# A chain of six transformer blocks on one core: the transposed maxima in bf16, joint additions, retention scores in one step, and value products in any free bank

## The chip, the cores and the metric

The kernel runs on one core of a Trainium2 chip. The metric is the device time of one execution in microseconds; lower is better.

## What is computed

The input `x` is 16 batch entries of 256 tokens by 256 features. Each entry goes through six stages, each followed by a layer normalisation. Reduced to what matters:

```python
x = LN(x + attn0(x))            # 16 heads mixed within each token (linear attention), then a GELU MLP
x = LN(x + window_attn(x, ctx)) # softmax attention, 16 heads of 16, |query - key| <= 64
x = LN(x + cells(x))            # six chained softmax attentions, 8 heads of 32
x = LN(x + retention(x))        # out = q . cumsum(k v^T), 16 heads, causal, no softmax
x = LN(x + cross_attn(x, ctx, mask))  # softmax attention, 16 heads of 16, masked keys
x = LN(x + fourier_ffn(x))      # one 256 x 256 matrix in effect
```

Every softmax attention is `exp(s - max(s))` over 256 keys, its sum, and its product with the values.

## The kernel before

**Entries and slots.** Up to four entries are in flight (`NS = 4`, `s = i % NS`), each with its own SBUF slots; an entry starts when the one four before it has ended. An entry is a list of steps (`entry_steps`, from line 147). Each step names its engine, a duration, the steps that it needs, what it takes of PSUM (`takes`) and what it gives back (`frees`).

**The order.** `program_plan` (from line 323) plays the steps of all 16 entries through in list order of priority (the older entry first, then the longer tail, shaken by random numbers from `SEEDS`), and writes down the order of every engine and the banks that each step gets. The chip then runs these five fixed orders; semaphores alone hold it together. The durations in the list serve only to write the order. Among the kinds in `takes`, "misc" is any free bank, "score" a pair of banks (neighbours if there are any), "kept" a pair whose first bank stays taken until "rest", "half" one of the two halves of the probability buffer `pt` in SBUF, "ctx" a bank that is held long. PSUM has eight banks (`BANKS`). Where a step lacks what it wants, steps of lower priority that want the same kind are held back too.

**Attention in quads.** Four heads are one unit, `heads(n)` (line 207): `n` 0 to 3 are windowed (kind x), 4 to 15 belong to the cells (kind c), 16 to 19 are the masked cross attention (kind y). The steps of a unit are:
- `s` on TensorE: scores, queries by keys, each head with 32 contraction rows in a row group of its own and in a bank of its own. VectorE takes the negated maxima into `nmx` (L1257, for kind x L1251).
- `split` on VectorE: each f32 maximum is cut into three parts whose upper halves are bf16 numbers (L1263, L1266).
- `nm` on TensorE (L898): two f32 transposes of `nmx`, 128 by 128. ScalarE copies the result to SBUF (L1472).
- `st` on TensorE: the scores again, keys by queries (L911), and onto them the maxima as a product of three rows of ones with the three bf16 parts (L915). ScalarE takes the exponential (L1488) into `pt`. For kind c VectorE adds the two key blocks (L1275), for kind x GpSimd cuts the band (L1658).
- `pv` on TensorE (L942, L949): values by probabilities, and the sums. It is written into the first bank of the pair that the second exponential was read from; the bank is "kept" for this from the start of `st`. ScalarE and VectorE normalise and end its use (L1281, L1285, L1291, L1293, L1503).

An f32 product is two records in the trace.

**Retention.** For each of two feature blocks `f` there are two half steps `rs` (L1021), `(f, 0)` and `(f, 1)`: two heads each, for both parities and two token blocks, eight products of 128 columns. VectorE multiplies each half by the causal mask into `pt` (L1335). Then `rpv` (L1032, L1038) multiplies by the values, into a "ctx" bank. `r_state` (L1004) comes ahead.

**Elsewhere.** `features` (L750) and `tokens` (L742) are the 256 by 256 projections, `transposes` (L735) the transposes of activations, L853 the first MLP product. GpSimd's L1638 and L1648 are the products of the first attention.

## Time and profile before

| | before |
|---|---|
| three runs | 3463.22, 3470.81, 3472.40 us; median 3470.81 |
| profiled execution | 3470.35 us, its span 3468.6 us, mean granted TensorE clock 0.967 |
| TensorE matmuls busy | 3157.1 us (91%), 30860 records |
| weight loads (beside them) | 2362.2 us (68%) |
| VectorE | 2319.2 us (67%) |
| ScalarE | 1695.7 us (49%) |
| GpSimd | 1202.3 us (35%) |
| DMA | 122.9 MB, 35 GB/s |

Busy time is the union of an engine's instructions. Matmuls are pipelined and overlap each other, so what one costs is read from the distance between starts, and not from its duration. After some 400 us of setup and filling, the trace repeats itself every 202 to 204 us, once per entry, until some 3150 us.

### The profile page before, as it was taken

What the parts mean: (1) busy time and instruction counts of PE and PEld (TensorE: products, weight loads), DVE (VectorE), ACT (ScalarE), POOL (GpSimd) and SP (SyncE); (2) the same over time, 40 slices, a digit from 0 to 9 for tenths busy, and PEclk for the clock granted to TensorE, in tenths of its full rate; (3) what the DMA queues carried; (4) which work ended last, traced back from release to release, by engine and by line L of the source; (5) the groups of instructions that cost most, each with busy time, mean ns of one, the idle gap of its engine ahead of it and who ended that gap; (6) DMA issues with size and microseconds to landing.
All of it is one profiled execution on the core that took longest, in us unless ns stands there. A gap on an engine that the chain in (4) does not pass through costs nothing.

```text
span 3468.6 us, 77951 instructions
## 1 busy us (share of the span) xinstructions
PE 3157.1 (91%) x30860; PEld 2362.2 (68%) x30860; DVE 2319.2 (67%) x5004; ACT 1695.7 (49%) x3492; POOL 1202.3 (35%) x1308
## 2 busy tenths in 40 slices
PE   6889999999999999999999999999999999998866
PEld 5766666777676667667667776766777666666654
DVE  6676667667585776858677676867667585565533
ACT  1245464545546454454645545464544546454532
POOL 6886016162341606234160523416162341000000
PEclk8899999999999999999999999999999999999986
DMA  6211010010101001010100101010010101000000
GB/s 221 71 56 35 19 35 29 26 47 17 50 23 38 29 26 47 17 47 26 38 29 26 47 17 47 26 38 29 26 47 17 47 26 30 22 16 8 16 4 4
DMA packets 123283, 122.90 MB, mean 35 GB/s; under 512 B 9776, under 2 KB 122672, under 8 KB 122800
## 3 DMA queue, kind: packets, MB, share of 16 engines
q1 hardware_dynamic: 122928, 117.91, 11.2%
q8 instruction: 254, 4.16, 0.5%
q14 instruction: 101, 0.83, 0.1%
HBM read 113.69 MB, written 4.19 MB: 34 GB/s over the span
## 4 chain that ended last, share of the span: by engine, by line
PE 60%; DVE 16%; POOL 9%; issue 7%; ACT 6%; DMA 1%; SPq 1%; POOLq 0%; DVEq 0%; ACTq 0%
PE banks L750 17%; PE banks L742 13%; PE banks L888 7%; DVE nmx L1257 6%; PE banks L911 5%; PE banks L942 4%; POOL work L1648 4%; POOL work L1638 4%; ACT work L1488 3%; PE banks L1021 2%; PE banks L735 2%; PE banks L853 2%; DVE work L1218 2%; PE banks L898 1%; PE banks L949 1%
## 5 line engine op out<-in xcount | busy, mean ns | idle before, releaser
L750 PE MATMUL banks<-work,weights 128*128 128x256 f32 x3584 | 862.0, 388 | 19.4 <-DVE work L1281 13.5
L750 PEld LDWEIGHTS banks<-work,weights 128*128 128x128 f32 x3584 | 667.6, 192 | 161.3 <-issue 51.0
L1257 DVE TENSOR_REDUCE nmx<-banks 128x4 f32<-128x1024 f32 (+1 forms) x527 | 605.0, 1188 | 209.7 <-PE banks L888 209.3
L1488 ACT ACTIVATE work<-banks 128x1024 f32<-128x1024 f32 (+2 forms) x699 | 595.7, 913 | 281.5 <-PE banks L915 279.2
L742 PE MATMUL banks<-weights,work 128*128 128x256 f32 x2688 | 651.0, 388 | 29.9 <-DVE work L1281 12.3
L742 PEld LDWEIGHTS banks<-weights,work 128*128 128x128 f32 x2688 | 501.3, 193 | 132.9 <-issue 43.4
L1648 POOL TENSOR_TENSOR work<-work 128x512 f32<-128x512 f32 x256 | 400.1, 1582 | 202.2 <-DVE work L1218 105.1
L911 PE MATMUL banks<-work 32*128 32x256 f32 (+1 forms) x5120 | 395.2, 395 | 39.7 <-DVE nmx L1257 15.4
L888 PE MATMUL banks<-work 32*128 32x256 f32 (+1 forms) x5120 | 359.9, 396 | 67.1 <-ACT work L1390 37.6
L1638 POOL TENSOR_TENSOR work<-work 128x512 f32<-128x512 f32 x256 | 346.8, 1380 | 51.1 <-DVE work L1209 28.6
L1692 POOL TENSOR_TENSOR work<-work,row 128x512 f32<-128x512 f32 x64 | 107.6, 1681 | 731.0 <-PE banks L735 731.0
L942 PE MATMUL banks<-work 128*32 128x256 f32 (+3 forms) x5632 | 331.5, 356 | 25.2 <-DVE nmx L1257 16.6
L1275 DVE TENSOR_TENSOR added<-work 128x1024 f32<-128x1024 f32 x192 | 272.2, 1423 | 116.3 <-ACT work L1488 98.0
L888 PEld LDWEIGHTS banks<-work 32*128 32x128 f32 x5120 | 239.5, 189 | 152.8 <-issue 102.6
L911 PEld LDWEIGHTS banks<-work 32*128 32x128 f32 x5120 | 216.1, 190 | 173.5 <-issue 88.8
L1390 ACT ACTIVATE work<-banks,cb 128x256 f32<-128x256 f32 x384 | 161.0, 472 | 224.0 <-PE banks L750 224.0
L942 PEld LDWEIGHTS banks<-work 128*32 128x32 f32 x5632 | 153.6, 109 | 164.2 <-issue 83.9
L1218 DVE TENSOR_REDUCE work<-work 128x32 f32<-128x512 f32 x256 | 174.0, 682 | 126.3 <-POOL work L1648 124.4
L1658 POOL TENSOR_SCALAR_AFFINE_SELECT work<-work 128x128 f32<-128x128 f32 (+1 forms) x512 | 158.6, 356 | 285.6 <-ACT work L1488 285.6
L1214 DVE TENSOR_REDUCE work<-work 128x32 f32<-128x512 f32 x256 | 172.0, 682 | 121.9 <-POOL work L1638 121.8
L1472 ACT ACTIVATE work<-banks 128x256 f32<-128x256 f32 x320 | 119.0, 385 | 130.4 <-PE banks L898 130.0
L1251 DVE CUSTOM_DVE_ANT_0 banks<-banks,band 128x192 f32<-128x192 f32 x512 | 164.9, 393 | 19.9 <-PE banks L888 19.6
(160 smaller groups left out, 3753.2 us busy)
## 6 DMA issues: line engine op xcount, KB each, us to landing
weights<-in_w_all SPq DMA_DIRECT2D x322, 256.0 KB, 2.7
work<-in_w_setup SPq DMA_DIRECT2D x41, 256.0 KB, 5.8
work<-in_ctx SPq DMA_DIRECT2D x32, 256.0 KB, 3.0
work<-in_x SPq DMA_DIRECT2D x16, 256.0 KB, 2.9
out<-work SPq DMA_DIRECT2D x16, 256.0 KB, 2.2
weights<-in_w_all SPq DMA_DIRECT2D x1, 3072.0 KB, 12.8
row<-in_rows SPq DMA_DIRECT2D x1, 1280.0 KB, 9.2
mrow<-in_mask SPq DMA_DIRECT2D x16, 32.0 KB, 3.3
```

The source lines that it names most:

```text
L742: ins = e.matmul(b[:, m * 256:m * 256 + 256], xin[:, k, m * P:m * P + P], wslot(w)[:, k, :], start=(k == 0 and (m == 0 or closed)) if star ...
L750: ins = e.matmul(b[:, m * 256:m * 256 + 256], wslot(w)[:, k, m * P:m * P + P], xin[:, k, :], start=(k == 0 and (m == 0 or closed)) if star ...
L888: ins = e.matmul(b[g // 2][g % 2][:, cc * 256:cc * 256 + kk.stop - kk.start], q[32 * g:32 * g + 32, f, cc * P:cc * P + P], k[32 * g:32 * g ...
L911: e.matmul(b[g // 2][g % 2][:, o], k[32 * g:32 * g + 32, f, kc * P:kc * P + P], q[32 * g:32 * g + 32, f, qq], start=True, stop=False, tile ...
L942: ins = e.matmul(b[32 * g:32 * g + 32, lo:hi], left, right[:, kc * 256 + lo - qq.start:kc * 256 + hi - qq.start], start=(kc == 0), stop=(k ...
L1214: e.tensor_reduce(mix, big1, AX, ALU.add).then_inc(*tell(vec[s], "mix", a, i))
L1218: e.tensor_reduce(q, big2, AX, ALU.add).then_inc(*tell(vec[s], "mix sum", a, i))
L1257: ins = e.tensor_reduce(nmax(s, n)[:, 2 * p + j:2 * p + end, :], b.rearrange("p j (c n) -> p j c n", c=NC)[:, :, :, 0:w], AX, ALU.max, neg ...
L1275: e.tensor_tensor(added[:, half], pt(half, 0, 4)[:, :, 0:S], pt(half, 0, 4)[:, :, S:2 * S], ALU.add).then_inc(*tell(vec[s], "added", a, i))
L1488: ins = e.activation(dst, b.rearrange("p j (c n) -> p j c n", c=NC)[:, :, :, 0:w], ACT.Exp)
L1638: e.tensor_tensor(big1, q.unsqueeze(2).broadcast_to([P, PH, NH, DH]), k.unsqueeze(1).broadcast_to([P, PH, NH, DH]), ALU.mult).then_inc(*te ...
L1648: e.tensor_tensor(big2, mix.unsqueeze(2).broadcast_to([P, PH, DH, NH]), v.unsqueeze(1).broadcast_to([P, PH, DH, NH]), ALU.mult).then_inc(* ...
```

## The change

Five edits:
- `nm`: the two f32 transposes become two bf16 products of the upper halves of `nmx` (a strided view) with a bf16 identity. The results are stored as bf16, densely.
- `st` of kinds c and y: the scores of both key blocks come first, and then each head has one addition of 512 columns (the maxima are read twice by a broadcast) where there were two of 256. For kind x the order stays. The first product of a bank alone carries the start flag.
- `st` takes two plain pairs; both banks of each are free after the exponential. `pv` takes any free bank as it starts, and its readers free that.
- `rs`: one step per feature block, four heads, sixteen products; it takes a half, two pairs and a "ctx" bank at once.
- The listed durations of six steps, and the five seeds, are others, so that the order of every engine and the banks are written anew.

```diff
-SEEDS = (271952, 450768, 66414, 843758, 204716)
+SEEDS = (452137, 292473, 324644, 23518, 278264)
...
-        maxed = [do("DVE", "s", (n, p), 1.13, b, frees=((b, p),)) for p in range(2)]
+        maxed = [do("DVE", "s", (n, p), 1.13 if kind != "x" else 1.21, b, frees=((b, p),)) for p in range(2)]
...
-        b = do("PE", "nm", n, 0.22, *maxed, *((st_done[n - 2],) if n >= 2 else ()), takes=("misc",))
+        b = do("PE", "nm", n, 0.16, *maxed, *((st_done[n - 2],) if n >= 2 else ()), takes=("misc",))
...
-        s = st_done[n] = do("PE", "st", n, 1.12 if kind != "x" else 1.0, nm, 
+        s = st_done[n] = do("PE", "st", n, 1.2 if kind != "x" else 1.08, nm, 
...
-                            takes=("score", "kept", "half"))
+                            takes=("score", "score", "half"))
...
-            e = [do("POOL", "band", (n, p), 1.0, e[p]) for p in range(2)]
+            e = [do("POOL", "band", (n, p), 1.22, e[p]) for p in range(2)]
         pv = do("PE", "pv", n, 1.3 if kind == "c" else 0.9, *e, *both, v,
-                frees=((s, 2),))
+                takes=("misc",), frees=((s, 2),))
         if par == 0:
-            part[n] = do("ACT", "part", n, 0.7, pv, frees=((s, "rest"),))
+            part[n] = do("ACT", "part", n, 0.7, pv, frees=((pv, 0),))
...
-        p0 = do("PE", "rs", (f, 0), 0.87, r_q_t, *((("PE", "rs", (f - 1, 0)),) if f else ()), takes=("half", "score", "ctx"))
-        m0 = do("DVE", "rs", (f, 0), 1.22, p0, frees=((p0, 1),))
-        p1 = do("PE", "rs", (f, 1), 0.87, p0, takes=("score",))
-        m1 = do("DVE", "rs", (f, 1), 1.22, p1, frees=((p1, 0),))
...
+        p = do("PE", "rs", f, 0.95, r_q_t, *((("PE", "rs", f - 1),) if f else ()), takes=("half", "score", "score", "ctx"))
+        m = [do("DVE", "rs", (f, j), 1.22, p, frees=((p, 1 + j),)) for j in range(2)]
...
+        def nmax_parts(s, n, c):
+
+            return small[s]["nmx"].bitcast(BF16)[:, n % 2, c].rearrange("p (n h) -> p n h", h=2)[:, :, 1]
...
         def stored_nmax(s, n):
-            return slot(s, NMT[quad(n)[0]])[:, n % 2, :]
+            return slot(s, NMT[quad(n)[0]])[:, n % 2, :].bitcast(BF16)[:, 0:S]
...
-                        ins = e.transpose(b[:, c * P:c * P + P], small[s]["nmx"][:, a % 2, c, :], ident[:, :])
+                        ins = e.matmul(b[:, c * P:c * P + P], nmax_parts(s, a, c), ident_bf[:, :], start=True, stop=True)
...
-                                     q[32 * g:32 * g + 32, f, qq], start=True, stop=False,
+                                     q[32 * g:32 * g + 32, f, qq], start=(kc == 0), stop=False,
...
+                    if kind != "x":
                         for g in range(4):
-                            ins = e.matmul(b[g // 2][g % 2][:, o], added_row[32 * g:32 * g + 3, :],
-                                           upper(stored_nmax(s, a))[32 * g:32 * g + 3, qq], start=False,
-                                           stop=True, tile_position=(32 * g, 0))
-                            if kc == NC - 1 and g == 1:
+                            ins = e.matmul(b[g // 2][g % 2].rearrange("p (c n) -> p c n", c=NC), ones_bf[32 * g:32 * g + 3, :],
+                                           stored_nmax(s, a)[32 * g:32 * g + 3, :].unsqueeze(1).broadcast_to([3, NC, S]),
+                                           start=False, stop=True, tile_position=(32 * g, 0))
+                            if g == 1:
...
-                    picked[:] = [home["exp", a, 1, i][0]]
-                    b = take("ctx", "norm", a, i)
+                    b = take("misc", "norm", a, i)
...
-                    b = take("score", "rm", f, p, i)
-                    if p == 0:
-                        take("ctx", "rout", f, i)
+                    book(i, f"r{a}")
+                    b = [take("score", "rm", a, 0, i), take("score", "rm", a, 1, i)]
+                    take("ctx", "rout", a, i)
                     for par in range(2):
                         for c in range(NC):
-                            for j in range(2):
-                                g = 2 * p + j
...
+                            for g in range(4):
```

## Rows read from the trace of the kernel before

**Rows 1.** The page: busy time by engine, and the chain that ended last.

```profile
PE 3157.1 (91%) x30860; PEld 2362.2 (68%) x30860; DVE 2319.2 (67%) x5004; ACT 1695.7 (49%) x3492; POOL 1202.3 (35%) x1308
...
PE 60%; DVE 16%; POOL 9%; issue 7%; ACT 6%; DMA 1%; SPq 1%; POOLq 0%; DVEq 0%; ACTq 0%
```

**Rows 2.** Busy time by stage: stretch, its length, then each engine, clock, DMA.

```profile
400.00:3150.00 2750.00, 2573.38 (x26040) 1914.74 (x26038) 1914.26 (x4170) 1431.37 (x2960) 927.34 (x1026) 0.99 0.11 31
3150.00:3469.00 319.00, 242.58 (x2244) 175.68 (x2244) 146.08 (x266) 122.82 (x249) 10.28 (x13) 0.86 0.03 8
...
1431.00:1633.00 202.00, 189.92 (x1903) 141.25 (x1902) 142.53 (x309) 105.20 (x218) 74.74 (x79) 0.98 0.11 33
```

**Rows 3.** TensorE's waits in the whole run: total us, times, longest.

```profile
PE banks L888 <- ACT work L1390: 37.6, 35, 2.3
...
PE banks L888 <- DVE nmx L1257: 24.1, 34, 1.5
PE banks L1021 <- DVE work L1335: 17.9, 13, 1.5
PE banks L942 <- DVE nmx L1257: 16.6, 13, 1.3
PE banks L911 <- DVE nmx L1257: 15.4, 34, 1.2
```

**Rows 4.** Groups by line and shape: busy, mean ns of one, idle before.

```profile
L898 PE MATMUL banks<-ident,nmx 128*128 128x128 f32 x640 | 124.4, 291 | 43.0 <-DVE nmx L1266 27.9 <-DVE nmx L1257 11.7 <-DVE nmx L1251 0.3
...
L898 PEld LDWEIGHTS banks<-ident,nmx 128*128 128x128 f32 x640 | 74.9, 143 | 109.2 <-issue 53.5 <-DVE nmx L1266 45.1
...
L915 PEld LDWEIGHTS banks<-work,ones_bf 3*128 3x128 bf16 x2048 | 64.3, 94 | 4.6
```

**Rows 5.** TensorE in order of time (start, us): transposes of maxima, what follows.

```profile
1525.85 0.60 PE L898 MATMUL banks<-ident,nmx 128*128 128x128 f32 x4
1526.29 3.62 PE L742 MATMUL banks<-weights,work 128*128 128x256 f32 x16
```

**Rows 6.** TensorE in order of time: the second half of an `st` step.

```profile
1530.49 0.61 PE L911 MATMUL banks<-work 32*128 32x256 f32 x8
1530.92 0.30 PE L915 MATMUL banks<-work,ones_bf 3*128 3x256 bf16 x4
1531.04 0.61 PE L911 MATMUL banks<-work 32*128 32x256 f32 x8
```

**Rows 7.** TensorE in order of time: retention scores at the full clock.

```profile
1229.85 1.05 PE L1021 MATMUL banks<-work 32*128 32x128 f32 x14
1230.63 0.48 PE L888 MATMUL banks<-work 32*128 32x256 f32 x2
1230.73 0.28 PE L1021 MATMUL banks<-work 32*128 32x128 f32 x2
1230.84 1.03 PE L888 MATMUL banks<-work 32*128 32x256 f32 x14
1231.80 0.44 PE L898 MATMUL banks<-ident,nmx 128*128 128x128 f32 x2
1233.72 3.33 PE L1021 MATMUL banks<-work 32*128 32x128 f32 x48 [1.48 <-DVE work L1335]
1236.98 0.71 PE L1032 MATMUL banks<-work 128*128 128x128 f32 x4
```

**Rows 8.** The same stretch by engine, and a later entry's at a lower clock.

```profile
1229.50:1237.00 7.50, 6.02 (x87) 5.00 (x85) 7.43 (x15) 0.77 (x3) 2.53 (x2) 1.00 0.11 37
...
1638.00:1643.00 5.00, 4.71 (x50) 4.28 (x51) 5.00 (x8) 0.00 (x0) 0.00 (x0) 0.73 0.00 0
...
1638.29 4.25 PE L1021 MATMUL banks<-work 32*128 32x128 f32 x48 [1.48 <-DVE work L1335]
1642.47 1.22 PE L1032 MATMUL banks<-work 128*128 128x128 f32 x4
```

**Rows 9.** VectorE's masking of retention scores, in order of time.

```profile
1232.32 1.26 DVE L1335 TENSOR_TENSOR work<-banks,causal 128x512 f32<-128x512 f32 x2
```

More of the change, by code:

```diff
@@ L361, in pick @@
                 found = [0] if long_held[0] < LONG else []
-            elif kind in ("score", "kept"):
+            elif kind == "score":
                 found = sorted(((u, v) for u in range(BANKS) for v in range(u + 1, BANKS) if bank_left[u] and bank_left[v]),
@@ L382, in mark @@
             bank[u[0]] = bank[u[1]] = is_free
-        elif kind == "kept":
-            bank[u[1]] = is_free
-            bank[u[0]] = False
-        elif kind == "rest":
-            bank[u[0]] = True
         elif kind == "misc":
@@ L905, in tensor @@
                     e.wait_ge(*when("nm", a, i))
-                    added_row = minus_bf if kind == "x" else ones_bf
                     for kc in range(NC):
@@ L1008, in tensor @@
                 elif op == "rs":
[L1009 to L1010 removed]
+                    if a == 0:
                         e.wait_ge(*when("r_q_t", i))
[L1012 to L1016 removed]
+                    book(i, f"r{a}")
+                    b = [take("score", "rm", a, 0, i), take("score", "rm", a, 1, i)]
+                    take("ctx", "rout", a, i)
                     for par in range(2):
                         for c in range(NC):
[L1019 to L1023 removed]
+                            for g in range(4):
+                                ins = e.matmul(b[g // 2][g % 2][:, par * S + c * P:par * S + c * P + P],
+                                               slot(s, XT)[32 * g:32 * g + 32, a, c * P:c * P + P],
+                                               slot(s, R_QT[par])[32 * g:32 * g + 32, a, c * P:c * P + P],
                                                start=True, stop=True, tile_position=(32 * g, 0))
[L1025 removed]
+                                if par == 1 and c == 1 and g == 1:
+                                    ins.then_inc(*tell(pe[s], "rs mm", a, 0, i))
+                    ins.then_inc(*tell(pe[s], "rs mm", a, 1, i))
                 elif op == "rpv":
```

24 lines of the change are left out of this document (10 added, 14 removed).

## The prediction

> **What bounds the kernel now.** I read the page's busy shares first. The reader is to see one engine far ahead of the others: TensorE's matmuls are busy for 3157 of 3468.6 us, 91%, and the chain that ended last lies on TensorE for 60% of the span, on VectorE for 16% [rows 1]. Then the busy time by stage: between 400 and 3150 us matmuls are busy for 2573 of 2750 us, 94%, and in one period of 202 us (one batch entry goes in and one comes out) for 189.9 us; VectorE has 142.5 us in the same period, ScalarE 105, GpSimd 75 [rows 2]. So a microsecond of TensorE work taken out of an entry should shorten the run by nearly a microsecond, as long as the 12 us of idle time in a period do not grow. In the last 319 us TensorE is busy for 243 only; there latency counts, not work. Last I read who ended TensorE's waits: no single cause is large, and the largest are inputs of a score product (37.6 us over the run), the row maxima that VectorE takes out of banks (24.1, 16.6 and 15.4 us ahead of three kinds of product), and the retention products' banks (17.9 us) [rows 3].
>
> The sum below is made against the profiled execution, 3470.35 us (span 3468.6); the median of the three runs is 3470.81, so they are the same to 0.5 us.
>
> **Transposes of the maxima.** There are 20 `nm` steps in an entry, 320 in all (640 records [rows 4]). Two such steps in a row start at 1525.85 and the next operation at 1526.29: 0.44 us, 0.22 us each [rows 5]. Each is two f32 transposes of 128 columns. The new step has two bf16 products of 128 columns. No row shows a bf16 product over the whole array. From below, the bf16 additions stream 4 products of 256 columns, on four row groups at once, in 0.12 us, so one product of 128 columns cannot be put at less than 0.06 us: 0.12 us a step [rows 6]. From above, the step stays at 0.22 us if its two weight loads set its pace: 143 ns is one f32 load now, and 94 ns one bf16 load of three rows [rows 4]. Two loads of 94 ns, half covered, give some 0.16 us. I take that, 0.06 us less a step: 320 x 0.06 = **19 us** (0 to 32). Nothing argues for a loss. The Trainium skill (TensorE: Matmul & The Clock Gate, Back-to-back issue gap) puts an isolated bf16 product of 128 columns at 55.6 ns; by that the step would be 0.11 us and the saving 35 us, and no row here shows it.
>
> ScalarE's copy of the result now writes bf16; I count nothing, since ScalarE is busy for 105 of 202 us [rows 2].
>
> **Joint additions.** In the 256 `st` steps of the kinds c and y, the products of one key block take 0.43 us (1530.49 to 1530.92) and its four additions 0.12 us [rows 6]. Afterwards there are two blocks of products, 0.86 us, and four additions of 512 columns. These cost 0.24 us if each costs twice one of 256, and 0.21 us if only the columns count (512 at 2.4 GHz). The step goes from 1.10 us to between 1.07 and 1.10. I take 0.02 us: 256 x 0.02 = **5 us** (0 to 8). The 64 steps of kind x keep all their instructions, and the dense bf16 maxima that they now read are no fewer columns.
>
> **Retention scores in one step.** Now there are four half steps per entry, each with two row groups. In the period at 1229 us the first starts at 1229.85 and gives way at 1230.73, 0.88 us; a score step and a transpose of other entries come between; then TensorE idles 1.48 us until VectorE's masking of the first half has emptied banks, and the other three halves take until 1236.98, 3.26 us [rows 7]. The joint step has the same columns on four row groups: 32 records of 128 columns, against 16 of 256 in a score step, of which the last 14 take 0.96 us (1230.84 to 1231.80) [rows 7]. I put it at 1.05 us. Pure work: 4 x 0.88 - 2 x 1.05 = 1.4 us an entry, 16 x 1.4 = **23 us**. Around it lie stalls: the idle 1.48 us (17.9 us over the run [rows 3]); 3.26 - 3 x 0.88 = 0.6 us by which the later halves are drawn out, 10 us over 16 entries; and in about nine entries the same three halves take 4.18 us (1638.29 to 1642.47) [rows 8], 0.9 us more, 8 us. In that stretch the granted clock is 0.73 in the mean, so partly at the lower of its two levels (1.2 GHz), after TensorE had idled 1.48 us and gone on with two row groups [rows 8]. Together 36 us. They do not all go. VectorE still has four maskings for each step, 2.5 us (two take 1.26 us) [rows 9], and is busy for 7.43 of the 7.50 us around it now [rows 8]; the second joint step must wait for banks that these empty, and is late by 2.5 us unless other entries' products fill that. I take a third: **12 us** (from -20 to 36; below nothing, because a step now claims four score banks and one for its output at once, five of eight).
>
> **Value product in any bank.** It has the same instructions, so no TensorE work moves. A bank that was kept from the start of `st` to the end of the normalisation is now free from the exponential to the value product, and the value product has to find one free. What covers it is that it claims one bank and not a pair, and that the normalisation empties it soon. If it waits instead, `co`, the next score step and all behind it on TensorE wait as well, and with them ScalarE's normalisation. The nearest rows are today's waits of products for maxima in banks, 16.6 and 15.4 us over the run [rows 3]. So I bound this between -30 us (most of rows 3's bank waits go) and +15 us (as many again come), and take 0.
>
> **The order.** All five engines' orders are written out anew with other costs and other seeds. Every step may move, weight streaming on SyncE's queue with it (its loads follow the starts of products), and GpSimd's bands and additions. No row prices that. TensorE's 12 us of idle time per period are what an order can win or lose; I allow 1 us a period either way, 15 us, and take 0.
>
> Sum: 19 + 5 + 23 + 12 = 59 us, 3470.35 - 59 = **3411 us**; 3390 to 3432 as this case's own range, from the order's 15 us and the transposes' bounds.
>
> **Rivals.** *VectorE bounds the retention stretch.* For: it is busy for 7.43 of 7.50 us there [rows 8], and its eight maskings, 5.0 us an entry, are not touched. Against: TensorE has products of three other entries to put in between, and VectorE has 59 us of slack in a period [rows 2]. Then only the 24 us of transposes and additions are won: 3446 us. The Trainium skill states this as a rule (TensorEngine Tiling (Array Packing), PSUM Bottleneck): tiling speeds up TensorE, and emptying PSUM may become the bottleneck.
>
> *More comes back.* If the freed bank removes half of the 56 us of waits on L1257, and the other 24 us of retention stalls go too: 3411 - 28 - 24 = 3359 us.
>
> *Everything is returned as idle time,* because the latency of one entry's chain (exponentials, sums, GpSimd's products) sets the period and not TensorE: 3470 us. Against it speaks 94% busy; for it that 40% of the chain is not on TensorE [rows 1, 2].
>
> *Slower: the five banks.* A joint step starts only when two pairs, one more bank and a half of the probability buffer are free together. Under the list order lower steps that want pairs are held back for it, and single banks go on being taken by others. This decides from 59 / 32 = 1.8 us of TensorE idle time per joint step on. Today a half step that wants two banks idles 1.48 us [rows 7]; were it VectorE's whole time for a step, 2.5 us, the bill is 32 x 2.5 = 80 us, and the run takes 3411 + 80 = 3491 us. Against: in the steady stretch TensorE nearly always finds something else.
>
> **How the numbers follow.** The forecast, 0.45. VectorE bounds retention, 0.20 (the row of 7.43 in 7.50 is strong but local). More comes back, 0.12. All returned, 0.10. Five banks or a worse order, 0.13. A measurement of this kernel tells about 0.3%, 10 us, from no change. Faster by more: 0.45 + 0.20 + 0.12 = 0.77; within: 0.10; slower: 0.13. The range goes from 3370, which leaves out half of "more comes back" (0.06), to 3470, above which lie the slower case and a little of "all returned" (0.13 to 0.15).
>
> **What would show it.** Of the transposes: `nm` steps 0.16 us apart, not 0.22. Of the additions: 1024 records of 512 columns, 0.21 to 0.24 us per four. Of retention: two blocks of 32 records, each about 1.05 us, and no idle 1.48 us ahead of them; were the rival right, products of retention would be preceded by idle time ended by VectorE's masking. Of the banks: value products with no wait for an eviction. Overall: matmuls busy for some 3110 us (3157 - 47), and idle time in a period still near 12 us. I am wrong if idle time grows by what the work shrinks, or if the order's share, put at 0, is larger than any of the terms.

## The result and the profile after

The change made the kernel slower.

| | before | after |
|---|---|---|
| median of the runs | 3469.39 us | 3507.49 us (3497.86 to 3515.63) |
| ratio to before | | 1.0108 [1.0085, 1.0132] |
| profiled execution, its span | 3470.35, 3468.6 us | 3515.63, 3513.9 us |
| mean granted TensorE clock | 0.967 | 0.957 |
| TensorE busy / idle in the span | 3157.1 / 311.5 us | 3127.5 / 386.4 us |

The forecast was 3411 us, with 3370 to 3470 as its range. The median lies 96 us above the one and 37 us above the other. The profiled execution after is the longest of its four, 8 us above their median, so differences between the two profiles are some 7 us larger than those between the medians (38.1 us).

The page of the kernel after, busy time and the chain that ended last, as [rows 1]:

```profile
PE 3127.5 (89%) x29836; PEld 2321.7 (66%) x29836; DVE 2362.6 (67%) x5022; ACT 1695.1 (48%) x3504; POOL 1189.7 (34%) x1308
...
PE 54%; DVE 19%; POOL 9%; issue 9%; ACT 6%; DMA 2%; SPq 1%; DVEq 0%; POOLq 0%; ACTq 0%
```

TensorE works 29.6 us less, and idles 74.9 us more; together 45.3 us, the difference of the two spans. In the chain its part falls from 60% to 54% of the span (some 2080 to 1900 us), VectorE's rises from 16% to 19% (some 555 to 670 us), and the part in which an engine waited for nothing that the profile shows rises from 7% to 9% (some 243 to 316 us). VectorE is also busy for 43.4 us more, though the change gives it no new work.

The busy time by stage, as [rows 2] (stretch, length, then busy time and instructions of TensorE, weight loads, VectorE, ScalarE and GpSimd, granted clock, DMA share, GB/s). The last one is a period of the kernel after:

```profile
400.00:3150.00 2750.00, 2490.61 (x24399) 1839.78 (x24398) 1911.12 (x4085) 1390.49 (x2895) 906.04 (x993) 0.97 0.11 31
...
1439.00:1646.00 207.00, 186.98 (x1835) 137.98 (x1834) 144.53 (x303) 105.44 (x219) 74.78 (x79) 0.98 0.11 32
```

So the time is lost in the steady stretch: there TensorE's idle time goes from 177 to 259 us. Between 825 and 2905 us the same retention step returns every 208.0 us in the mean, where it returned every 202.6 us; a period has 20 us of idle time and not 12.

TensorE's groups of the kernel after, with the idle time just ahead of them and what ended it, as the first line of [rows 4]:

```profile
L891 PE MATMUL banks<-ident_bf,nmx 128*128 128x128 bf16 x640 | 88.1, 226 | 82.2 <-DVE nmx L1254 47.9 <-DVE nmx L1263 22.7 <-ACT work L1485 6.8
...
L1016 PE MATMUL banks<-work 32*128 32x128 f32 x1024 | 45.9, 326 | 30.6 <-DVE work L1332 22.6 <-DVE nmx L1254 8.1
```

Ahead of the `nm` steps TensorE now idles for 82.2 us, where it was 43.0 us [rows 4]: the very step that became cheaper has 39 us more idle time ahead of it. Ahead of retention scores it is 30.6 us, for 18 before [rows 3].

### The profile page after: what moved, and what is told of

The parts are those of the page before. It is cut to its first block, busy times and chain, and to the rows that moved or that the text cites. A ratio compares the mean times of both kernels' runs of the same rounds, so it can differ in the third digit from the quotient of the medians.

```text
span 3513.9 us, 75891 instructions
## 1 busy us (share of the span) xinstructions
PE 3127.5 (89%) x29836; PEld 2321.7 (66%) x29836; DVE 2362.6 (67%) x5022; ACT 1695.1 (48%) x3504; POOL 1189.7 (34%) x1308
## 4 chain that ended last, share of the span: by engine, by line
PE 54%; DVE 19%; POOL 9%; issue 9%; ACT 6%; DMA 2%; SPq 1%; DVEq 0%; POOLq 0%; ACTq 0%
PE banks L743 14%; PE banks L735 12%; DVE nmx L1254 6%; PE banks L903 6%; PE banks L881 5%; PE banks L941 5%; POOL work L1645 5%; POOL work L1635 3%; ACT work L1485 3%; DVE work L1195 2%; PE banks L846 2%; DVE added L1272 2%; PE banks L728 2%; PE banks L948 1%; DMA mrow<-in_mask 1%
## 5 line engine op out<-in xcount | busy, mean ns | idle before, releaser
L743 PE MATMUL banks<-work,weights 128*128 128x256 f32 x3584 | 848.4, 386 | 12.3 <-DVE work L1278 6.5
L1254 DVE TENSOR_REDUCE nmx<-banks 128x4 f32<-128x1024 f32 (+1 forms) x545 | 605.9, 1154 | 242.4 <-PE banks L881 240.8
L1485 ACT ACTIVATE work<-banks 128x1024 f32<-128x1024 f32 (+3 forms) x711 | 599.5, 899 | 265.7 <-PE banks L915 238.3
L735 PE MATMUL banks<-weights,work 128*128 128x256 f32 x2688 | 671.8, 397 | 44.3 <-DVE work L1278 28.7
L735 PEld LDWEIGHTS banks<-weights,work 128*128 128x128 f32 x2688 | 509.7, 196 | 159.8 <-issue 51.8
L1645 POOL TENSOR_TENSOR work<-work 128x512 f32<-128x512 f32 x256 | 407.3, 1606 | 36.2 <-DVE work L1215 19.1
L881 PE MATMUL banks<-work 32*128 32x256 f32 (+1 forms) x5120 | 356.6, 397 | 61.3 <-ACT work L1485 28.2
L903 PE MATMUL banks<-work 32*128 32x256 f32 (+1 forms) x5120 | 369.2, 398 | 40.4 <-ACT work L1469 18.3
L1635 POOL TENSOR_TENSOR work<-work 128x512 f32<-128x512 f32 x256 | 359.7, 1414 | 118.4 <-DVE work L1211 103.2
L1272 DVE TENSOR_TENSOR added<-work 128x1024 f32<-128x1024 f32 x192 | 271.2, 1412 | 164.7 <-ACT work L1485 161.0
L941 PE MATMUL banks<-work 128*32 128x256 f32 (+3 forms) x5632 | 334.2, 359 | 45.4 <-ACT work L1485 24.9
L881 PEld LDWEIGHTS banks<-work 32*128 32x128 f32 x5120 | 241.4, 190 | 154.2 <-issue 103.3
L903 PEld LDWEIGHTS banks<-work 32*128 32x128 f32 x5120 | 237.0, 190 | 146.8 <-issue 88.7
L1689 POOL TENSOR_TENSOR work<-work,row 128x512 f32<-128x512 f32 x64 | 89.2, 1394 | 608.9 <-PE banks L728 608.8
L1469 ACT ACTIVATE work<-banks 128x256 bf16<-128x256 f32 x320 | 121.5, 388 | 251.4 <-PE banks L891 251.3
L1211 DVE TENSOR_REDUCE work<-work 128x32 f32<-128x512 f32 x256 | 171.1, 678 | 55.0 <-POOL work L1635 54.8
L1677 POOL MEMSET work<- 128x512 f32 x16 | 8.4, 525 | 554.9 <-PE banks L1035 554.9
```

The lines of the kernel that those rows point to most:

```text
L735: ins = e.matmul(b[:, m * 256:m * 256 + 256], xin[:, k, m * P:m * P + P], wslot(w)[:, k, :], start=(k == 0 and (m == 0 or closed)) if star ...
L743: ins = e.matmul(b[:, m * 256:m * 256 + 256], wslot(w)[:, k, m * P:m * P + P], xin[:, k, :], start=(k == 0 and (m == 0 or closed)) if star ...
L881: ins = e.matmul(b[g // 2][g % 2][:, cc * 256:cc * 256 + kk.stop - kk.start], q[32 * g:32 * g + 32, f, cc * P:cc * P + P], k[32 * g:32 * g ...
L903: e.matmul(b[g // 2][g % 2][:, o], k[32 * g:32 * g + 32, f, kc * P:kc * P + P], q[32 * g:32 * g + 32, f, qq], start=(kc == 0), stop=False, ...
L941: ins = e.matmul(b[32 * g:32 * g + 32, lo:hi], left, right[:, kc * 256 + lo - qq.start:kc * 256 + hi - qq.start], start=(kc == 0), stop=(k ...
L1211: e.tensor_reduce(mix, big1, AX, ALU.add).then_inc(*tell(vec[s], "mix", a, i))
```

## The experiments

Two theories stood against each other at first. *The mechanics:* the joint retention step, the banks or the bf16 products cost more than forecast. *The order:* the edits are worth what the sum says, but the orders that are written out anew are worse by more. The median of the kernel before lay between 3468.35 and 3471.66 us in each series of measurements below, so times of different series can be compared to some 3 us. Some kernels below change `SEEDS` alone, and so only the written order; their computation stays the same. For each the table further down gives the makespan as well, the end of the play-through that `program_plan` itself comes to.

**The cheaper products alone, in the order of before.** The bf16 transposes and the joint additions are put into the kernel before; the list of steps, its durations and the seeds stay, so every engine keeps its order.

```diff
-    ins = e.transpose(b[:, c * P:c * P + P], small[s]["nmx"][:, a % 2, c, :], ident[:, :])
+    ins = e.matmul(b[:, c * P:c * P + P], nmax_parts(s, a, c), ident_bf[:, :], start=True, stop=True)
...
-    q[32 * g:32 * g + 32, f, qq], start=True, stop=False,
+    q[32 * g:32 * g + 32, f, qq], start=(kc == 0), stop=False,
...
-    ins = e.matmul(b[g // 2][g % 2][:, o], added_row[32 * g:32 * g + 3, :],
+    ins = e.matmul(b[g // 2][g % 2].rearrange("p (c n) -> p c n", c=NC), ones_bf[32 * g:32 * g + 3, :],
```

> The kernel before with the order of every engine and all banks held as they were; only the products of nm (bf16) and st (joint additions) are those of the change. Theory A, the new order lost the time and the products are cheaper as forecast: 24 to 40 us less than before, 3430 to 3446 us, with nm steps 0.13 us apart in place of 0.22. Rival B, the new products themselves cost time (a lower granted clock, a drain ahead of bf16): 3470 us or more. Rival C, the saved work turns into waits whatever the order: 3460 to 3475 us with more idle time on TensorE.

Measured: 3468.78 us, ratio 0.9995 [0.9982, 1.0008]. The page and the steady stretch of this kernel:

```profile
PE 3134.8 (91%) x29836; PEld 2334.6 (67%) x29836; DVE 2317.9 (67%) x5004; ACT 1695.9 (49%) x3492; POOL 1204.1 (35%) x1308
...
400.00:3150.00 2750.00, 2553.11 (x25154) 1891.56 (x25152) 1913.22 (x4172) 1430.22 (x2957) 928.86 (x1026) 0.98 0.11 31
```

TensorE's busy time falls by 22.3 us, 20.3 of them in the steady stretch, where as much idle time takes its place. The 24 us of these two terms are worth nothing in this order. In a fixed order the engine cannot take other work when its next input has not arrived. That is the result of the rival "everything is returned as idle time", for these two edits in a held order; that the latency of one entry's chain is the reason, as that rival says, is not shown. The clock moved as well: the mean granted clock is 0.961 to 0.963 in the ten runs and 0.962 to 0.968 in those of the kernel before beside them, and in the stretch shown it is 0.98 where it was 0.99 [rows 2]. The two edits do not explain the loss either, so it lies in the retention step, the banks or the order.

**The seeds exchanged.** The kernel before gets the seeds of the kernel after, and the other way round.

```diff
-SEEDS = (271952, 450768, 66414, 843758, 204716)
+SEEDS = (452137, 292473, 324644, 23518, 278264)
```

> The kernel before with the five new seeds and nothing else: the same instructions in another order. Theory A (an order is worth tens of microseconds): the makespan that the order writer itself comes to is 3490.2 in place of 3359.5, so some 130 us slower, about 3600 us. Rivals B and C, for which the order is nothing: within 15 us of before, 3455 to 3485 us.

> The changed kernel with the five old seeds. Theory A: the order writer comes to 3465.4 in place of 3373.7, so some 90 us slower than the changed kernel, about 3600 us. Rival D, the claims of the joint retention step and of the value product are what costs, whatever the seeds: within 15 us of the changed kernel, 3490 to 3525 us.

**No seeds.** Both kernels with `SEEDS = ()`, where nothing shakes the priorities: the first order that the rule alone gives.

> The kernel before with no seeds: the partner of the changed kernel with no seeds, which took 3560 us (1.027 of before). The order writer comes to 3457.6 here and to 3435.9 there. Theory A, the change shortens the run where neither order was picked: slower than that partner, 3570 to 3620 us. Theory D, its claims cost as much as its instructions save: 3560 us or less.

> The changed kernel with no seeds at all, so that the order follows the plain tails and nobody has picked it. To be read against the kernel before with no seeds, e4. The order writer comes to 3435.9 here and 3457.6 there. Theory A: some 3570 us, and 20 to 60 us less than e4. Rival D: as slow as e4 or slower.

**Seeds sought anew for both.** For each kernel 2100 orders were written, and the one with the shortest makespan was run.

> The changed kernel with eight other seeds, found as the best of 2100 orders by the makespan that the order writer itself comes to: 3326.5 where the recorded seeds come to 3373.7 and the kernel before to 3359.5. On the five kernels run so far, 1 us of that makespan is about 1.3 us on the chip. Theory A, the change is sound and its seeds were not: 3425 to 3460 us, faster than both. Theory D, the claims of the new steps cost on the chip what the writer does not see: 3480 us or more.

> The kernel before with three other seeds, the best of 2100 orders by the writer's makespan (3375.9), the same effort as for the changed kernel, whose best was 3326.5 and took 3453 us. Theory A: 3480 to 3520 us, slower than the kernel before, whose recorded seeds (3359.5) are a lucky find, and slower than the changed kernel with its searched seeds. Theory D: 3455 us or less.

Measured, sorted by makespan (us):

| list of steps | seeds | makespan | time | ratio to before |
|---|---|---|---|---|
| after | best of 2100 | 3326.5 | 3453.34 | 0.996 [0.9946, 0.9975] |
| before | its own | 3359.5 | 3469.39 | 1 |
| after | its own | 3373.7 | 3507.49 | 1.0108 [1.0085, 1.0132] |
| before | best of 2100 | 3375.9 | 3519.30 | 1.0132 [1.0114, 1.0149] |
| after | none | 3435.9 | 3560.31 | 1.0266 [1.0227, 1.0305] |
| before | none | 3457.6 | 3598.67 | 1.0361 [1.0343, 1.0379] |
| after | those of before | 3465.4 | 3613.42 | 1.0417 [1.0382, 1.0451] |
| before | those of after | 3490.2 | 3640.69 | 1.0495 [1.0467, 1.0523] |

The searched and unshaken runs came out in the ranges expected; of the exchanges, for which I had some 3600 us each, that of the kernel before is 41 us slower than that. Four things follow. The order alone moves the time by 171 us (3469 to 3641), and I had allowed it 15. Seeds chosen for one list did harm in the other: either kernel is slower with the other's seeds than with none. The makespan ranks all eight as the chip does; over the whole table 163.7 us of makespan are 187.4 us on the chip. And the kernel before had an unusually good order: 2100 orders of its list hold none with so short a makespan (3375.9 against 3359.5), and the best of them takes 49.9 us longer than its own.

The loss can be split along these runs, in two ways. Without seeds the change saves 3598.67 - 3560.31 = 38.4 us. Its own seeds bring the kernel before 3598.67 - 3469.39 = 129.3 us, and the kernel after only 3560.31 - 3507.49 = 52.8 us, 76.5 us less. -38.4 + 76.5 = 38.1 us, which is the result. With one search of the same length for each, the change saves 3519.3 - 3453.3 = 66 us; counted from there the two kernels' own seeds make 104 us of difference. So the edits are worth 38 to 66 us in orders that they had an even chance in, and the orders that the two kernels came with lose 76 to 104 us. That the sum had 59 does not confirm its terms: below, the cheaper products give 0 and 11 us where it had 24.

By the rival of the five banks the new list would be the slower one in both pairs, since the joint step claims its banks in every order of it. It is the faster in both. That the claims cost something within the 38 and 66 us is not excluded.

**Where part of the order's idle time comes from: the split of the maxima.** In the trace after, one `split` instruction of VectorE that usually takes 0.17 us takes 3.11 us. VectorE, GpSimd and TensorE in order of time (start, duration, engine, line, operation, and for TensorE the idle time ahead and its end):

```profile
1367.54 0.68 DVE L1211 TENSOR_REDUCE work<-work 128x32 f32<-128x512 f32 x1
1368.13 3.11 DVE L1260 TENSOR_TENSOR nmx<-nmx 128x8 f32<-128x8 f32 x1
1371.28 0.18 DVE L1263 TENSOR_TENSOR nmx<-nmx 128x8 f32<-128x8 f32 x1
1371.37 1.22 DVE L1254 TENSOR_REDUCE nmx<-banks 128x4 f32<-128x1024 f32 x1
...
1367.30 1.49 POOL L1645 TENSOR_TENSOR work<-work 128x512 f32<-128x512 f32 x1
1368.76 2.45 POOL L1635 TENSOR_TENSOR work<-work 128x512 f32<-128x512 f32 x2
...
1372.73 0.37 PE L891 MATMUL banks<-ident_bf,nmx 128*128 128x128 bf16 x2 [3.75 <-DVE nmx L1254]
```

GpSimd multiplies in three instructions back to back from 1367.30 to 1371.21, and the 8-column subtraction ends only then. The maxima of the next unit (L1254) stand behind it on VectorE and free a bank at 1372.59; `nm` starts at 1372.73, after TensorE has idled for 3.75 us. The first reduction, 0.68 us, runs beside GpSimd without delay. Seven periods of the steady stretch have such a gap of 3.7 to 3.8 us. In four others the same instruction gets its turn between two of GpSimd's, the second one is held instead, and the gap is 2.1 to 2.4 us:

```profile
1577.71 0.71 DVE L1260 TENSOR_TENSOR nmx<-nmx 128x8 f32<-128x8 f32 x1
1578.46 1.17 DVE L1263 TENSOR_TENSOR nmx<-nmx 128x8 f32<-128x8 f32 x1
...
1576.87 1.52 POOL L1645 TENSOR_TENSOR work<-work 128x512 f32<-128x512 f32 x1
1578.34 2.47 POOL L1635 TENSOR_TENSOR work<-work 128x512 f32<-128x512 f32 x2
```

TensorE's clock behind the gap at 1369 us (same columns as above):

```profile
1368.00:1371.00 3.00, 0.99 (x17) 0.58 (x15) 3.00 (x2) 0.00 (x0) 3.00 (x3) 1.00 0.00 0
1371.00:1374.00 3.00, 1.26 (x4) 0.98 (x5) 2.96 (x5) 0.38 (x1) 0.21 (x1) 0.57 0.00 0
1374.00:1377.00 3.00, 3.00 (x8) 2.37 (x7) 2.93 (x7) 0.00 (x0) 0.05 (x1) 0.50 0.00 0
```

The granted clock is 1.00 while the engine falls idle, and 0.57 and 0.50 (the lower level, 1.2 GHz) in the next two stretches, although TensorE is busy for all of the last one.

To take the suspected cause away, the two subtractions are replaced by instructions of the same size that read one operand, so that the lower two parts of the maxima stay zero (`nmx` is set to zero at the start); this leaves out the lower two parts of every maximum. All five orders are held. It is done in the kernel after and in the kernel before.

```diff
-    e.tensor_tensor(nmax(s, a, 1), nmax(s, a, 0), nmax_upper(s, a, 0), ALU.subtract)
+    e.tensor_reduce(nmax(s, a, 1), nmax(s, a, 2).unsqueeze(3), AX, ALU.max)
...
-    e.tensor_tensor(nmax(s, a, 2), nmax(s, a, 1), nmax_upper(s, a, 1), ALU.subtract)
+    e.tensor_reduce(nmax(s, a, 2), nmax(s, a, 1).unsqueeze(3), AX, ALU.max)
```

> The changed kernel, its order held; the two small VectorE instructions that split the maxima (two SBUF inputs, 0.17 us alone, up to 3.11 us while GpSimd multiplies) become instructions with one SBUF input. Leaves out: the two lower parts of the maxima, which stay zero, so that the maximum that is subtracted is rounded to bf16. Theory P, VectorE and GpSimd share a port and this makes part of the 43 us that VectorE is busier: the longest split falls from 3.1 to 0.2 us, the 3.75 us gap of TensorE in each period goes, the low-clock stretch behind it too, 25 to 60 us less than the changed kernel: 3447 to 3482 us. Theory O, the order's waits alone cost: 3500 to 3510 us.

> The same edit in the kernel before, its order held, leaving out the same lower parts of the maxima. Theory P: the splits are held far less here (longest 1.27 us), so 0 to 12 us less than before, 3458 to 3470 us, and the changed kernel gains at least twice as much from the edit. Theory O: 3465 to 3472 us, and both gain the same.

Measured: after 3457.73 us, ratio 0.9974 [0.996, 0.9989], 49.8 us less than the kernel after; before 3434.18 us, ratio 0.9917 [0.9892, 0.9942], 35.2 us less than the kernel before. The two splits as groups (busy us, mean ns, idle ahead): first in the kernel after, then with one operand; and the same line's shortest, median and longest in ns in both:

```profile
L1263 DVE TENSOR_TENSOR nmx<-nmx 128x8 f32<-128x8 f32 x320 | 83.0, 260 | 11.0
L1260 DVE TENSOR_TENSOR nmx<-nmx 128x8 f32<-128x8 f32 x320 | 80.3, 251 | 5.8 <-issue 0.3
...
L1260 DVE TENSOR_TENSOR nmx<-nmx x320: 159/170/3140, 140.3 to 3484.9; 128x8 f32<-128x8 f32 x160
```

```profile
L1263 DVE TENSOR_REDUCE nmx<-nmx 128x8 f32<-128x8 f32 x320 | 54.0, 169 | 11.0
L1260 DVE TENSOR_REDUCE nmx<-nmx 128x8 f32<-128x8 f32 x320 | 51.9, 162 | 5.9 <-issue 0.3
...
L1260 DVE TENSOR_REDUCE nmx<-nmx x320: 151/161/171, 146.6 to 3436.0; 128x8 f32<-128x8 f32 x160
```

A median of 170 and a longest of 3140 ns become 161 and 171: the holds are gone, 57 us of VectorE's time, for 50 us of the run. The gaps of 3.7 us in the steady stretch are gone with them, and `nm` has 47.1 us of idle time ahead of it where it had 82.2:

```profile
L891 PE MATMUL banks<-ident_bf,nmx 128*128 128x128 bf16 x640 | 87.4, 225 | 47.1 <-DVE nmx L1263 19.0 <-DVE nmx L1254 17.9 <-ACT work L1485 6.8
```

Of the 48.9 us between the two profiled spans, TensorE's idle time makes 25.8 and its busy time 23.1 (3127.5 to 3104.4 us for the same products), while the mean clock rises from 0.957 to 0.966.

In the kernel before the same two lines are busy for 128.8 us, so the holds were there too and smaller, and taking them away is worth 35 us. I had put that at 12 us at most, and expected the changed kernel to gain at least twice as much: two misses. The difference, 14.5 us, is the part of the 38 us that this one contention explains, and it is loose: by the ratios the gains are 46 and 29 us, and the intervals allow some 13 us either way. The written order knows nothing of the contention, and the new one puts more splits beside GpSimd's products: 40 of the 640 take over 0.3 us, before 20. But the holds do not rank orders. In the searched order, 54 us faster, the splits are held longer still, 170.2 us for 163.3:

```profile
L1260 DVE TENSOR_TENSOR nmx<-nmx 128x8 f32<-128x8 f32 x320 | 107.6, 336 | 9.4
L1263 DVE TENSOR_TENSOR nmx<-nmx 128x8 f32<-128x8 f32 x320 | 62.6, 196 | 11.1 <-DVE nmx L1260 0.2
```

**The low clock at the second retention step.** In the kernel after the second joint step runs at the lower clock in nine of the 16 entries, here for its whole length:

```profile
1242.44 1.17 PE L1016 MATMUL banks<-work 32*128 32x128 f32 x32 [0.74 <-DVE nmx L1254]
1243.55 0.28 PE L891 MATMUL banks<-ident_bf,nmx 128*128 128x128 bf16 x2
1245.55 2.09 PE L1016 MATMUL banks<-work 32*128 32x128 f32 x32 [1.72 <-DVE work L1332]
1247.57 0.80 PE L1029 MATMUL banks<-work 128*128 128x128 f32 x2
```

The first takes 1.11 us (1242.44 to 1243.55), the second 2.02 us, after 1.72 us of idle time that VectorE's masking ended. To see what the low clock costs, TensorE is given extra products into the output's bank ahead of each joint step, so that it does not stand idle there.

```diff
...
+    spare = take("ctx", "rout", a, i)
+    for _ in range(3 if a else 1):
+        e.matmul(spare[:, 0:S], slot(s, XT)[:, a, 0:P], slot(s, XT)[:, a, 0:S], start=True, stop=True)
...
```

> The changed kernel, its order held, with f32 products of 128x256 that nobody reads ahead of the two joint retention steps, one before the first and three before the second, in the bank that the step's output gets later: they fill the gaps of 0.7 and 1.7 us in which TensorE waits there for VectorE. Theory G, the gaps bring the lower clock for what follows: the second joint step takes 1.1 us in place of 1.9 to 2.1 in every entry, the low-clock time in the steady stretch falls from 150 to about 110 us, and the run is 5 to 20 us faster than the changed kernel, 3487 to 3502 us. If the clock does not answer to this: the same or up to 15 us slower, by the products themselves where the gaps are short.

Measured: 3506.39 us, ratio 1.0113 [1.0098, 1.0128]; no different from the kernel after. The clock did come back. The stretch around the second step and the step itself:

```profile
1238.00:1244.00 6.00, 5.63 (x108) 4.50 (x108) 5.86 (x14) 0.38 (x1) 0.00 (x0) 1.00 0.01 3
...
1241.26 1.17 PE L1020 MATMUL banks<-work 32*128 32x128 f32 x32
1242.36 0.71 PE L1033 MATMUL banks<-work 128*128 128x128 f32 x4
```

The second step takes 1.10 us (1241.26 to 1242.36) at a granted clock of 1.00, all 32 joint steps now take 1.10 or 1.11 us, and the run's mean clock rises from 0.957 to 0.967 (0.963 to 0.967 in its four runs, where the kernel after has 0.957 to 0.964). The time stays, where I had expected 5 to 20 us less. VectorE is busy for 5.86 of these 6.00 us, which fits that the stretch waits for it and that a faster TensorE there ends nothing sooner. So the low clock at this step did not make the kernel slower. For the rest of the run that is not shown: the extra products are work themselves (64, at 0.50 us each where three take 1.49 us), the mean clock between 400 and 3150 us came back in part only (0.97, now 0.98; before 0.99), and within the kernel after the slowest run has the lowest clock (3515.63 us at 0.957) and the fastest the highest (3497.86 us at 0.964).

**Do cheap products pay where the order suits them?** *Work* (Theory W below): they pay once the holds on VectorE are gone. *Held order* (Theory H): they pay only in an order that was written for them. For the one, the edits of the first experiment are put on the kernel before with one-operand splits (lower two parts left out here too). For the other, the searched order of the kernel after is held, and the old f32 transposes and the two additions of 256 columns are put back under it.

```diff
-    ins = e.matmul(b[:, c * P:c * P + P], nmax_parts(s, a, c), ident_bf[:, :], start=True, stop=True)
+    ins = e.transpose(b[:, c * P:c * P + P], small[s]["nmx"][:, a % 2, c, :], ident[:, :])
...
-    ins = e.matmul(b[g // 2][g % 2].rearrange("p (c n) -> p c n", c=NC), ones_bf[32 * g:32 * g + 3, :],
+    ins = e.matmul(b[g // 2][g % 2][:, o], added_row[32 * g:32 * g + 3, :],
```

> The kernel before, its order held, with the bf16 transposes and joint additions and with the splits of the maxima that have one SBUF input (leaves out the two lower parts of the maxima). The one-input splits alone took 3434 us, the cheaper products alone 3469. Theory W, the products' saving was hidden because transposes wait for VectorE's splits, which GpSimd holds: 3405 to 3425 us. Theory H, an order written for the old durations has no place where this saving counts, held splits or not: 3428 to 3440 us.

> The changed kernel with the searched seeds (3453 us), its order held, but with the f32 transposes and the two additions of the kernel before: everything else of the change stays. Theory H, the products' cost counts in an order that was written for the cheap ones: 20 to 40 us slower than 3453, 3473 to 3493 us. If the cheaper products are worth nothing in any order: 3445 to 3465 us, and the change's gain is all of the retention step and the banks.

Measured: 3439.17 us, ratio 0.9917 [0.9895, 0.9939], where the same kernel without them has 3434.18; and 3464.77 us, ratio 0.9989 [0.9976, 1.0002], where the searched order with the new products has 3453.34. In the order written for the old list they are worth nothing even without holds, so *Work* fails. In the searched order of the new list they are worth 11.4 us, about half of the 24 us that the sum gave them; the runs do not overlap (3449.84 to 3456.5 against 3457.89 to 3470.25 us). But 3464.77 us is below the 3473 to 3493 of *Held order* and in the range that I had given for products worth nothing in any order. And the new list is not one of cheaper products throughout: it has `nm` at 0.16 for 0.22 and `st` at 1.20 for 1.12. So what is shown is that the same edit is worth nothing in one order and some 11 us in another; that the list's durations make the difference is not.

One rival was not taken apart from this: in each of the three pairs the kernel with the cheaper products has the lower clock in its profiled run (0.963 for 0.967 in the first experiment, 0.965 for 0.974 and 0.959 for 0.962 here), so part of the saved work may have gone into slower products.

**The best of both.** The searched order with one-operand splits; and then the split step taken out of the list and the code altogether, `nm` waiting for the maxima themselves, at 0.14 us in the list, with the best of some 12000 orders. Both leave out the lower two parts of the maxima.

```diff
-        maxed = [do("DVE", "split", n, 0.36, *maxed)]
-        b = do("PE", "nm", n, 0.16, *maxed, *((st_done[n - 2],) if n >= 2 else ()), takes=("misc",))
+        b = do("PE", "nm", n, 0.14, *maxed, *((st_done[n - 2],) if n >= 2 else ()), takes=("misc",))
```

> The changed kernel with the eight searched seeds and the splits of the maxima with one SBUF input (leaves out the lower two parts of the maxima, which stay zero). If the port's share and the order's add up: 3453 less 30 to 50 us, 3405 to 3425 us. If the search already avoids what the port costs: 3440 us or more.

> The changed kernel without the split at all: the transposes start from the maxima, the lower two parts stay zero (left out), the step is gone from the list, and the seeds are the best of some 12000 orders, makespan 3290.8. By 1.3 us on the chip for each us of makespan against the kernel before: 3380 us; 3370 to 3410 us, faster than both kernels.

Measured: 3398.54 us, ratio 0.9781 [0.9761, 0.98]; and 3396.05 us, ratio 0.9775 [0.9756, 0.9794], makespan 3290.8. One-operand splits are worth 54.8 us on top of the searched order, more than I had expected (30 to 50). The second kernel is faster than before by more than 2%, the first is just at that mark; both are over 3% below the kernel after. The second brings next to nothing over the first, though its makespan is 36 us shorter: the list prices a split at 0.36 us, and on the chip the two take 0.33 us once nothing holds them. So between these two the makespan did not tell the time; what became of those 36 us is open.

## Why the prediction was wrong

**The order, put at 0 and bounded by 15 us, is the step that failed.** "TensorE's 12 us of idle time per period are what an order can win or lose; I allow 1 us a period" takes the idle time that a good order leaves as a measure of what a bad one can cost. It bounds what a better order could still win, and says nothing of what a worse one loses. Measured, the order is worth 76 to 104 us between the two kernels with their own seeds, and 171 us for one kernel with other seeds. The prediction's last sentence named this case ("if the order's share, put at 0, is larger than any of the terms"); it is the one that came, with "idle time grows by what the work shrinks": busy time fell by 29.6 us and idle time grew by 74.9.

**The premise that a microsecond of TensorE work is nearly a microsecond of time failed as well.** It rests on 94% busy. Taking 22 us of work out without moving anything gave 0.9995 [0.9982, 1.0008]. The 94% is an average over five fixed orders that wait for one another, and in both kernels only 54 to 60% of the chain lies on TensorE.

**A reading of the waits was wrong.** The prediction calls 37.6 us and then the maxima and the retention banks TensorE's largest waits. Two of the three largest are left out there, behind two small VectorE instructions, the scaling of the layer normalisation and the split:

```profile
PE banks L735 <- DVE work L1198: 29.0, 7, 14.1
PE banks L898 <- DVE nmx L1266: 27.9, 21, 4.5
```

So the prediction never asked what these two cost. The waits alone would not have told: with one-operand splits the second is still 25.9 us, and the kernel before gains 35 us all the same.

**The terms, one by one.**
- *Transposes, 0.22 to 0.16 us.* Right in kind, the size too small. One step starts at 1237.78 and what follows at 1237.91: 0.13 us, at the lower bound (0.12) and not at the value taken. At 0.09 us less a step the term would be 29 us; with the additions that makes 34 us, and TensorE's busy time fell by 22.3 us in the first experiment.

```profile
1237.78 0.29 PE L891 MATMUL banks<-ident_bf,nmx 128*128 128x128 bf16 x2
1237.91 0.61 PE L728 MATMUL banks<-ident,work 128*128 128x128 f32 x4
```

- *Joint additions, 0.21 to 0.24 us per four.* Right: 0.22 us (1504.26 to 1504.48), in 1024 records.

```profile
1504.26 0.40 PE L915 MATMUL banks<-work,ones_bf 3*128 3x512 bf16 x4
1504.48 1.04 PE L903 MATMUL banks<-work 32*128 32x256 f32 x16
```

- *Retention work, 1.05 us a step.* 1.11 us at the full clock, so 4 x 0.88 - 2 x 1.11 = 1.3 us an entry and not 1.4. The second step of an entry takes 1.70 to 2.02 us in the nine entries in which it meets the low clock.
- *Retention stalls, a third of 36 us gained.* Wrong in sign. The idle time that VectorE's masking ends ahead of these products went from 17.9 us [rows 3] to 22.6, and 8.1 us behind maxima came on top. This is the mechanism of the rival of VectorE as the bound, which I gave 0.20, though its time (3446 us) is 61 us too low; the sentence of the Trainium skill (TensorEngine Tiling (Array Packing), PSUM Bottleneck) that it was weighed with holds here: the masking is what the second step waits for, 1.72 us in the entry shown. The extra products fit it: TensorE's speed at that step was worth nothing.
- *Value product in any bank, 0 between -30 and +15 us.* Its waits behind maxima fell from 16.6 us [rows 3] to 2.5, and those of the second scores from 15.4 us [rows 3] to 7.3. But value products now wait 24.9 us for the exponentials (before 7.7), and `nm` 47.9 us behind maxima (before 11.7). The waits moved on; which of it is the bank and which the order was not taken apart.

TensorE's waits in the kernel after (us in total, times, longest), as [rows 3]:

```profile
PE banks L891 <- DVE nmx L1254: 47.9, 26, 3.8
PE banks L728 <- DVE work L1195: 36.0, 17, 14.2
...
PE banks L941 <- ACT work L1485: 24.9, 44, 1.1
PE banks L891 <- DVE nmx L1263: 22.7, 16, 4.2
PE banks L1016 <- DVE work L1332: 22.6, 14, 1.8
```

- *Matmuls busy for some 3110 us.* 3127.5: 29.6 us less work, where 47 were forecast.

**The five banks,** the rival that ended on the other side, gave a time near the result (3491 us) for a reason that does not hold: without seeds and with searched seeds the new list is faster than the old, by 38 and 66 us. That the rival's number lies 16 us from the median is luck.

**What stays open.** The retention step and the free bank were not run apart, so how the 38 to 66 us divide between them is not shown. "Best of 2100" is one draw for each kernel, and 66 us have that draw in them. The listed durations changed together with the code, and no run tells the two apart. Some 14.5 of the 38 us, give or take 13, are holds on the splits; the rest of what makes the new order worse is known only as its makespan, 14.2 us longer than that of before, and the part of the clock in it is open.

## What to carry to other kernels

Where every engine runs an order that a planner wrote, a change of the planner's list is two changes: price the edit with both orders sought with equal effort, and give the order a range taken from a few other seeds, not from today's idle time. The planner's own makespan is cheap, and it ranked eight orders here without a mistake; it knows nothing of what the list leaves out, such as holds (50 us at the same makespan). And a small instruction between two engines' queues is worth a look at its longest, not its median: instructions of 0.17 us, some of them held for up to 3.1 us, cost 50 us of the run, more than the cheaper products gave in any order.

## What the runs showed of the hardware

**A two-operand VectorE instruction is held while GpSimd works, and sometimes does not get its turn between GpSimd's instructions.** The subtraction of 8 columns waited through the rest of one product of 1.49 us and two more, 2.45 us together, that GpSimd ran without a gap; 3.11 us for 0.17. In other periods of the same trace it got its turn after the first product, 0.71 us at 1577.71; what decides between the two is not known. Of the 40 splits that take over 0.3 us, 39 end within 0.1 us after a GpSimd instruction ends. Reductions with one operand in SBUF ran beside them at 0.68 us, and as a replacement for the subtraction never took more than 172 ns. The Trainium skill (SBUF — State Buffer, "SBUF: two separate sides") states the lock: a VectorE instruction with two SBUF operands and a GpSimd instruction that reads SBUF exclude each other for their whole length. The trace agrees. By the same section whichever starts first keeps the pair for its instruction, which alone would bound a hold here by the rest of one product, under 1.5 us; the measured 3.1 us is the longer, and the measurement decides. The hold works the other way too: 38 of the 256 products of L1635 take over 1.5 us (median 1.27), and 37 of them overlap VectorE's addition of L1272, which has two operands.

**The scaling of the layer normalisation is held in the same way.** Its group in the kernel after, against 97.7 us and 428 ns in the kernel before:

```profile
L1195 DVE TENSOR_SCALAR work<-work,mv,rstd 128x256 f32<-128x256 f32 x256 | 145.0, 608 | 15.5 <-ACT rstd L1396 15.4
```

It is the same instruction 256 times, 47 us longer in all, and one-operand splits leave it as it is (144.1 us). Most of the 256 keep to the median of 411 ns; 55 take over 0.6 us, before 8, and 54 of the 55 end within 0.2 us after a GpSimd instruction ends. Two in a row:

```profile
1389.59 1.02 DVE L1195 TENSOR_SCALAR work<-work,mv,rstd 128x256 f32<-128x256 f32 x1
1390.53 1.61 DVE L1195 TENSOR_SCALAR work<-work,mv,rstd 128x256 f32<-128x256 f32 x1
...
1388.20 2.26 POOL L1635 TENSOR_TENSOR work<-work 128x512 f32<-128x512 f32 x1
1390.42 1.57 POOL L1645 TENSOR_TENSOR work<-work 128x512 f32<-128x512 f32 x1
```

The first ends 0.15 us after L1635 does, the second 0.15 us after L1645. No run takes this hold away, so what it costs is not shown; waits of TensorE behind it (L728) are 36.0 us in the kernel after and were 29.0.

**Full clock regained, nothing gained.** A stretch brought from the lower level to the full clock by extra products (mean clock of the run 0.957 to 0.967) left the time where it was, 3507 and 3506 us. The mean granted clock alone ranks kernels badly: 0.959 went with 3456.5 us (searched seeds, kernel after), 0.969 with 3522.8 us (searched seeds, kernel before). Within one kernel the two go together: the kernel after with one-operand splits took 3450.66 us at 0.969 and 3469.25 us at 0.964. Which of them moves the other is not shown.
